# Cached values loaded half by SyncE's queue, page by page, and half by GpSimd's gather

## The reference

```
q = rope(rmsnorm(x Wq^T));  k = rope(rmsnorm(x Wk^T));  v = x Wv^T     # 32 query heads, 8 key heads, D = 128
kc = k_cache[block_table];  vc = v_cache[block_table]                    # 16 pages of 32 keys: 512 cached keys
k_all = concat(kc, k);      v_all = concat(vc, v)                        # 544 keys
scores = q k_all^T / sqrt(128), masked where a cached key's number >= cache_seqlens
x = x + (softmax(scores) v_all) Wo^T
```

## Time and profile before

| what | value |
|---|---|
| median of 3 runs | 2318.11 us (2316.63 to 2318.87) |
| profiled execution | 2318.34 us, span 2316.4 us, mean granted clock 0.992 |
| busy share of the span | PE 98%, PEld 84%, DVE 74%, ACT 56%, POOL 50% |
| attention stage | about 720 to 1954 us |
| moved in all | 501.70 MB, mean 217 GB/s |
| q1 (SyncE's queue) | 366.44 MB, 48.5% of 16 engines' span |
| q0 (GpSimd's queue) | 134.23 MB, 16.3% |

### The profile page before, as it was taken

One profiled execution on the slowest core, in us unless ns is written; L12 is line 12 of the kernel. 1 busy time (PEld: TensorE's weight loads), 2 busy tenths in 40 slices (PEclk: granted clock), 3 DMA queues, 4 the chain that ended last, 5 costly groups with the idle time before them and its releaser, 6 DMA issues. The chain is left out here.

```text
span 2316.4 us, 52250 instructions
## 1 busy us (share of the span) xinstructions
PE 2260.5 (98%) x16384; PEld 1949.5 (84%) x16384; DVE 1705.4 (74%) x3504; ACT 1297.3 (56%) x2643; POOL 1146.9 (50%) x1218
## 2 busy tenths in 40 slices
PE   6898999999998999999999999999999998999999
PEld 6877777777776999999999999999999997888887
DVE  8861788888877888888888888888888886422121
ACT  6733888888886555555555555555555555311110
POOL 4200454544445777777777777777777773000000
PEclk9999999999998999999999999999999999999999
DMA  6533343434448888888888888888888885543442
GB/s 265 208 110 89 89 131 123 125 119 127 132 146 278 289 285 285 286 287 287 291 292 286 289 292 288 291 287 297 286 295 286 292 286 193 199 127 108 128 127 63
DMA packets 451816, 501.70 MB, mean 217 GB/s; under 512 B 95863, under 2 KB 390775, under 8 KB 443416
## 3 DMA queue, kind: packets, MB, share of 16 engines
q1 hardware_dynamic: 414872, 366.44, 48.5%
q0 software_dynamic: 36864, 134.23, 16.3%
HBM read 408.21 MB, written 92.34 MB: 216 GB/s over the span
## 5 line engine op out<-in xcount | busy, mean ns | idle before, releaser
L1275 ACT ACTIVATE att_probs<-att_probs,att_low 128x544 f32<-128x544 f32 x512 | 383.5, 749 | 517.7 <-DVE att_low L1363 447.2
L1171 POOL TENSOR_TENSOR att_probs<-att_probs,att_inverse 128x512 f32<-128x512 f32 x512 | 536.1, 1047 | 272.7 <-DVE att_inverse L1376 268.3
L1232 PE MATMUL att_o<-att_probs_t,att_values 128*128 128x128 f32 x4096 | 541.1, 275 | 1.4 <-DMA att_values<-L_cond_v_cache,att_v_rows_of 1.1
L1363 DVE CUSTOM_DVE_ANT_0 att_probs<-att_score,att_mask,att_batch_cols 128x544 f32<-128x544 f32 x512 | 399.7, 781 | 136.2 <-PE att_score L1197 96.5
L1232 PEld LDWEIGHTS att_o<-att_probs_t,att_values 128*128 128x128 f32 x4096 | 497.6, 192 | 1.8 <-DMA att_values<-L_cond_v_cache,att_v_rows_of 1.3
L1372 DVE COPY att_probs_t<-att_turn 128x512 f32<-128x512 f32 x512 | 350.7, 685 | 1.2 <-PE att_turn L1212 1.2
L1157 POOL DMA_INDIRECT att_values<-L_cond_v_cache,att_v_rows_of x256 | 284.1, 1110 | 82.3 <-POOL att_v_rows_of L1153 50.1
L1212 PE MATMUL att_turn<-ident,att_probs 128*128 128x128 f32 x2048 | 311.3, 275 | 1.2 <-POOL att_probs L1171 0.8
L984 POOL TENSOR_TENSOR proj_q_out<-proj_by_cos,proj_by_sin 128x512 f32<-128x512 f32 x128 | 187.8, 1467 | 216.6 <-DVE proj_by_sin L910 216.6
L1212 PEld LDWEIGHTS att_turn<-ident,att_probs 128*128 128x128 f32 x2048 | 244.6, 141 | 33.0 <-POOL att_probs L1171 1.4
L841 PE MATMUL proj_proj<-x3t_hi,proj_w_hi 128*128 128x512 f32 x640 | 255.1, 399 | 6.7 <-DVE proj_w_lo L895 6.7
(11 more groups left out here) (156 smaller groups left out, 4152.3 us busy)
## 6 DMA issues: line engine op xcount, KB each, us to landing
keys_first<-L_cond_k_cache SPq DMA_DIRECT2D x512, 128.0 KB
att_keys_raw<-L_cond_k_cache SPq DMA_DIRECT2D x512, 128.0 KB
q_t<-proj_q_out SPq DMA_DIRECT2D x32, 1024.0 KB, 5.4
o_t<-att_heads_out SPq DMA_DIRECT2D x64, 512.0 KB, 6.8
out_o_raw<-o_t SPq DMA_DIRECT2D x31, 1024.0 KB, 5.3
queries_first<-q_t SPq DMA_DIRECT2D x32, 512.0 KB
att_queries_raw<-q_t SPq DMA_DIRECT2D x32, 512.0 KB
maps_even<-L_cond_weight SPq DMA_DIRECT2D x8, 1024.0 KB, 12.2
```

Of the source, the lines that this page charges most:

```text
L1171: nc.gpsimd.tensor_tensor(probs[:, k, 0:L], probs[:, k, 0:L], inverse[:, k:k + 1].to_broadcast([P, L]), ALU.mult).then_inc(probs_ready, 1)
L1232: last = nc.tensor.matmul(o, values[j][:, t, h * D:(h + 1) * D], probs_t[m % 2][:, t * P:(t + 1) * P], start=(t == 0), stop=False, skip_gr ...
L1275: nc.scalar.activation(probs[:, k, :], probs[:, k, :], ACT.Exp, bias=low[k][:, 0:1], scale=-1.0, accum_out=total[k][:, 0:1]).then_inc(exp_ ...
L1363: nc.vector.tensor_tensor_reduce(out=probs[:, k, :], in0=score_ps[:, LEFT:LEFT + KEYS], in1=mask[j][:], scale=batch_cols[j][:, h:h + 1], s ...
```

## The change

The cached values of a batch come in two halves. Blocks 0 and 1 (pages 0 to 7 of the batch) are loaded by SyncE, a DMA of 128 KB for each page into 32 partitions, with a read of 8 page numbers ahead of them. Blocks 2 and 3 are still gathered by POOL, with two indirect DMAs, now at heads 3 and 4. SyncE's function loads the value pages and the new values of a batch; in the loop it stands before the keys instead of behind them. PE waits for both halves. The semaphore counts follow.

```diff
+    HALF = PPT // 2
+    VLD = 16 * (PPT - HALF)
+    VPLD = 16 * HALF * PPT
...
-            def load_new_values(v, b, done, first):
+            def load_values(v, b, done, first):
+
+                table_sb = first_pages if first else pages_sb
+                _, pages = nc.values_load_multi_w_load_instructions(
+                    table_sb[0:1, bass.ds(b * NPP, HALF * PPT)], engines=(mybir.EngineType.SP,), min_val=0, max_val=PAGES - 1,
+                    skip_runtime_bounds_check_because="VectorE has put every page number between 0 and PAGES - 1")
                 if not first:
                     sp.wait_ge(pages_loaded, 16)
                     sp.wait_ge(o_done, done * HK)
+                for n in range(HALF * PPT):
+                    t, c = divmod(n, PPT)
+                    sp.dma_start(values[v][c * PSIZE:(c + 1) * PSIZE, t, :],
+                                 v_cache[bass.ds(pages[n], 1)].rearrange("n k h d -> (n k) (h d)")).then_inc(v_pages_loaded[v], 16)
                 sp.dma_start(new_values[v].rearrange("p h d -> p (h d)"),
...
-            load_new_values(0, 0, 0, True)
+            load_values(0, 0, 0, True)
             sp.dma_start(pages_sb[:], table.rearrange("(o b) n -> o (b n)", o=1)).then_inc(pages_loaded, 16)
             load_keys(1, 1, 0, True)
-            load_new_values(1, 1, 0, True)
+            load_values(1, 1, 0, True)
...
             load_keys(0, 2, 1, False)
+            load_values(0, 2, 1, False)
             load_keys(1, 3, 1, False)
-            load_new_values(0, 2, 1, False)
             store(0, 0)
             with sp.Fori(2, PAIRS) as i:
+                load_values(1, i * 2 - 1, i * 2 - 2, False)
                 load_keys(0, i * 2, i, False)
-                load_new_values(1, i * 2 - 1, i * 2 - 2, False)
                 store(1, i - 2)
+                load_values(0, i * 2, i * 2 - 1, False)
                 load_keys(1, i * 2 + 1, i, False)
-                load_new_values(0, i * 2, i * 2 - 1, False)
                 store(0, i - 1)
-            load_new_values(1, B - 1, B - 2, False)
+            load_values(1, B - 1, B - 2, False)
...
-                    if 3 <= h < 3 + PPT and not (last_pair and j == 1):
+                    if 3 <= h < 3 + PPT - HALF and not (last_pair and j == 1):
...
-                        load((j + 1) % 2, i * 2 + (j + 1), h - 3)
+                        load((j + 1) % 2, i * 2 + (j + 1), HALF + h - 3)
...
                     pe.wait_ge(v_loaded[j], back * VLD + VLD)
+                    pe.wait_ge(v_pages_loaded[j], back * VPLD + VPLD)
```

More of the change, by code:

```diff
@@ L1014, in stage_attention @@
     KLD = 16 * (NPP + 2)
-    VLD = 16 * PPT
+    HALF = PPT // 2
+    VLD = 16 * (PPT - HALF)
+    VPLD = 16 * HALF * PPT
     NLD = 16
@@ L1062, in stage_attention @@
         v_loaded = a_.sem("v_loaded", 2)
+        v_pages_loaded = a_.sem("v_pages_loaded", 2)
         new_loaded = a_.sem("new_loaded", 2)
@@ L1151, in load @@
             def load(v, b, t):
-                if t == 0:
+                if t == HALF:
                     nc.gpsimd.tensor_copy(v_rows_of[v][:], v_index[:, bass.ds(b, 1), :].rearrange("p b t -> p (b t)")).then_inc(index_ready, 1)
@@ L1177, in pair @@
                                                 inverse[:, heads].unsqueeze(2).to_broadcast([P, GH, S]), ALU.mult).then_inc(group_ready, 1)
-            for t in range(PPT):
+            for t in range(HALF, PPT):
                 load(0, 0, t)
```

## The result

The changed kernel takes 2327.27 us in the median of six runs (2321.19 to 2328.17), the kernel before 2318.47 us beside it. The ratio is 1.0035 with a 95% interval of 1.0025 to 1.0045: slower by 0.35%, 6 to 10 us, where 40 were forecast. The profiled execution took 2321.19 us with a span of 2319.3 us, 2.9 us more than before's; it was the fastest of the six.

The account below looks back on a forecast made before the run. PE was taken to bound the kernel until SyncE's round exceeded its 19.05 us: 2318.34 + 3 (start) + 60 x 0.62 (SyncE's excess) = 2358 us, range 2316 to 2415.

Parts of the forecast that it names:

- What bounds the kernel: Attention stage: PE's own work sets 19.05 us a batch; SyncE waits 4.68 us of it, occupied for 14.37.
- SyncE's round: Steady loop: SyncE's work per batch grows from 14.37 to 19.67 us, 0.62 over PE's 19.05, for 60 rounds.
- the term for the start: Stage start: batch 1's keys and queries issue later behind value pages, PE loses time: +3 us, bounds 0 and +8.
- as a sum that is nothing: SyncE's loop: new values move behind the value pages, the wait behind the queries falls to the store, net zero.
- The read: SyncE's page-number reads: added one behind a load 1.1 us; the one behind the store 0.2 us shorter with 8 numbers.
- My sum by that floor: Alternative estimate, added read at the skill's floor near 600 ns: round 19.37 us, 0.32 too many, 2340 us.
- Rival A: SyncE's loop still fits as both reads fall to 0.97 us: round 18.6 us, 2321 or 2310 us; chance 0.20.
- Rival B: SyncE's loop: both page-number reads stay long, round 20.97 us, 1.92 too many, 2436 us; chance 0.15.
- Rival C: DMA transfers become the bound, 32-partition pages taking twice the gathers' time: 2333 us if SyncE fits; chance 0.08.
- PE's added wait: PE's wait for value pages before a batch's products: pages issued some 20 us ahead, so zero cost.
- the o_done condition: SyncE's wait before the value pages for PE's last products: met over 3 us early once SyncE is late, zero cost.
- GpSimd: Two of four gathers removed per batch; GpSimd is not the bound, so counted zero, bounds 0 and -8 us.

Follow-up runs that it names:

- the half-gather run: The kernel before without its third and fourth gather from batch 2 on, SyncE's instructions untouched: 2317.78 us, ratio 0.9999.
- three quarters on SyncE: The changed kernel with twelve value pages on SyncE and one gather, instead of eight and two: 2406.86 us, ratio 1.0383.
- the second one: The changed kernel run again unchanged as control, for a second median and second profile: 2324.14 us, ratio 1.0032.
- the run with both batches gathered: The changed kernel with batches 0 and 1 gathered whole by GpSimd as before the change: 2316.84 us, ratio 0.9997.

## Why the prediction was wrong, point by point

**What bounds the kernel** was right: PE before and after, with SyncE's slack of 4.68 us as the resource that the change spends.

**SyncE's round** is the step that failed. The kernel did get slower, as forecast, but not by this step, which was to bring 37 of the 40 us and brought none; that the time went the forecast way is luck, since the loss is made in the term for the start, put at 3 us. I summed 14.37 + 4.3 + 0.1 + 1.1 - 0.2 = 19.67 us. The means over 850 to 1800 us, before and after:

| term, us a batch | forecast | measured |
|---|---|---|
| 8 value pages | +4.3 | +3.88 |
| added read, behind a load | +1.1 | +0.99 |
| read behind the store | -0.2 | -0.70 (2.04 to 1.33) |
| 16 keys | 0 | -0.66 (8.59 to 7.93) |
| new values and store | 0 | -0.79 (1.54 to 0.75) |
| new keys and queries | 0 | -0.03 |
| register arithmetic and gaps | +0.1 | +0.64 |
| sum | +5.3 | +3.33 |

Every term but the last came out below the forecast. The biggest I had written off with the words "as a sum that is nothing": the wait of the issues behind the queries would only move to the store. It went, and the half-gather run shows that two gathers fewer are enough for that: with SyncE's own order untouched, new values and store lose 0.68 us, most of this term, and the keys 0.2 of their 0.66; the other 0.45 of the keys is open. It is not the load of the DMA engines as such, since in the changed kernel the DMA engines are fuller than before (93%) and the issues are short all the same. The old sum carried waits that were no cost of SyncE's own but came from the gathers beside it, and the change takes half of them away.

**The read** was half seen. It is long behind the store and 0.97 behind a load, as I took it. What I missed is that it can be short again when it starts right behind the store's end: in the changed kernel every other one begins 0.04 us behind it and takes 521 to 542 ns, and those between, across the turn of the loop, begin 0.5 us behind it and take 1838 to 2389. The floor near 600 ns of which the Trainium skill speaks (DMA: Bandwidth & Descriptors, Latency and other measured facts), and which I had weighed and set aside, is near the short kind and no floor for it (521 ns at the least, with 8 numbers); those behind a load take 967 ns and more. My sum by that floor also left out the 0.2 us taken off for the 8 numbers; with it the round would have been 19.17 us and not 19.37. Why 0.5 us of distance makes 1.7 us of difference is not known; with three quarters on SyncE the close ones took 748 to 1726 ns for 12 numbers, and in the kernel before reads that began 0.15 us behind the store took as long as those 0.49 behind it, so it is not the distance alone.

**Rival A**, that SyncE still fits, is what happened, and its start-only time of 2321 us is 6 below the median (3 below the second one). It was to decide at 2.35 us for both reads; they took 2.32. That they met this bound is luck: the reads did not fall to 0.97 each, as A had it, and most of the room came from other terms. By the measured terms the true point is 19.05 - (17.71 - 2.32) = 3.66 us, so A had far more room than the 0.20 I gave it. **Rival B** is refuted for the read behind the load: in no run did one take more than 1.06 us in the steady part. **Rival C** has its mechanism and not its effect. The two queues from 1001 to 1039 us, changed kernel, beside the earlier trace rows:

```profile
q1 hardware_dynamic: 8238, 8.84, 75.9%
q0 software_dynamic: 576, 2.10, 18.8%
```

The 2.03 MB that moved to SyncE's queue take 23.0% of the engines, 11.3% a MB, against 7.6% for the gathers before: half as much again, not twice, and 5% short of full. A part of this is crowding and not the pages' own cost, since the gathers that stayed went from 7.6 to 9.0% a MB too. With pages over 128 partitions q1 is 74.0% for 8.93 MB, so the number of partitions makes only a small part of it.

**The start** was forecast at +3 with bounds 0 and +8; it is 5.6 to 6.2 (6.1 to 7.0 in the second profile). The issue of the queries moved by 4.7 us instead of 5.5. The landing was taken as 4.5 us from a store's row and from bytes, while the rows at hand said 6.4: issued by 731.99, split at 738.36 on their arrival. After, it is 6.8 (735.55 to 742.37). So the split is 5.1 us late and not 3.6, 1.1 us of it absorbed (1.3 forecast), PE 4.1. The clock adds 2.1, which I had not counted at all: of the 6.8 us at 1.2 GHz PE worked through the last 4.7, which at 2.4 GHz would have been half as long. Batch 2's queries cost nothing, as forecast. The gain from the gathers' wait that goes (1.1 us) was in fact a new wait of 1.3 us for the queries' low part, the limit that I had named.

**PE's added wait and the o_done condition:** zero each, as forecast. **GpSimd** was put at zero with a bound of -8 us, and it gave 0.6 us: that much of the start's loss comes back once between batches 20 and 30. In the kernel before, PE waits there 0.4 us for GpSimd's multiply (at 1254.6 us, one of the two waits of the earlier trace rows) and the batch is 0.5 us longer. Every kernel here whose loop has four gathers shows two such waits between 850 and 1800 us, every one with two gathers shows one.

## What to carry to other kernels

When work goes onto an engine's queue, its slack is to be measured in what the engine needs by itself: durations that contain waiting on other traffic (the same instruction at 0.34 and at 1.05 us is the sign) can shrink when the change moves that traffic, and the sum should be made at both sizes. A queue that has slack in the loop often has none at the stage's start, and there every issue put ahead of the first critical load is paid nearly in full (keys 4.9 us later, PE 4.1), and 32 bytes in place of each 128 KB page cost about the same. Where PE will stand idle for some microseconds, look for the granted clock behind it and count that too.

## What the runs showed of the hardware

- SyncE's read of page numbers took 0.97 us (16 numbers) behind the issue of a load and mostly over 2 us (median 2.2 with the DMA engines at 82%, 2.4 at 70%) behind that of an output store; 0.53 us (8 numbers) where it began 0.04 us behind the store's end.
- A DMA of 128 KB whose address is in a register takes 0.49 to 0.54 us of SyncE's time in the steady part, arithmetic included. Eight of them at the head of the stage took 3.88 us, and eight of 32 bytes in the same place 3.24: a four-thousandth of the bytes saves a sixth.
- The issue of the new values, behind the queries, took 0.34 to 1.87 us in the kernel before. Half the gathers fewer brought it and the store from 1.54 to 0.86 us a batch. In the changed kernel they take 0.75 us, though the DMA engines are 93% busy instead of 82%.
- Where PE stood idle for 4.8 to 5.8 us at the start (six profiles), its clock fell to 1.2 GHz and stayed there for 6.8 us, which cost 2.0 to 2.8 us more; where it stood idle for 2.6 us at the same place, the clock stayed at 2.4 GHz. The length of one idle time does not settle it: at about 733 us the half-gather run fell to 1.2 GHz for 3.4 us after 1.8 us of idle PE, and the run with both batches gathered stayed at 2.4 GHz after 3.0 us.
